# The first attention of a two-layer kernel rebuilt: weight look-up on TensorE, low parts of q and k made once and placed by DMA

## The reference, cut to what matters

```python
xt = jnp.transpose(x, (0, 2, 1))
q = xt @ Wq.T                                    # B, T=256, D=128; 8 heads of 16
qh = q.reshape(B, T, NH, dk).transpose(0, 2, 1, 3)
scores = scale * jnp.einsum('bhqd,bhkd->bhqk', qh, qh)
logits = (scores * cmask + (1.0 - cmask) * NEG) * rmask     # NEG = -1e30
attn = jax.nn.softmax(logits, axis=-1)
ctx = jnp.einsum('bhqk,bhkd->bhqd', attn, qh)
out = ctx.reshape(B, T, D) @ Wo.T                # transposed back, feeds the feed-forward
w = lut[idx]                                     # 16 entries; gate, up (688x256) and down (256x688)
h = silu(x @ w_gate.T) * (x @ w_up.T);  x = x + h @ w_down.T
```

## Time and profile before

| what | value |
|---|---|
| median of three runs | 783.47 us |
| profiled execution: time, span | 785.27 us, 783.5 us |
| PE, PEld busy | 628.1 us (80%), 364.8 us (47%) |
| DVE busy | 503.9 us (64%) |
| ACT, POOL busy | 373.6 us (48%), 214.3 us (27%) |
| mean granted clock of PE | 0.876 |

### The profile page before, as it was taken

The page is one execution under the profiler, slowest core; times in us unless marked ns, Lnnn a source line. Parts: engine busy times, 40 slices in busy tenths (PEclk is TensorE's granted clock), DMA queues, the critical chain, the costliest instruction groups (busy, mean ns, idle before and its releaser), DMA issues. The chain is left out here.

```text
span 783.5 us, 14597 instructions
## 1 busy us (share of the span) xinstructions
PE 628.1 (80%) x4411; PEld 364.8 (47%) x4443; DVE 503.9 (64%) x1050; ACT 373.6 (48%) x686; POOL 214.3 (27%) x243
## 2 busy tenths in 40 slices
PE   3588888787888879999956787788628999999993
PEld 1134444444444435555533454454414666666662
DVE  2589888999888875333336999999852333333331
ACT  1356766656766654243336777777502222222220
POOL 3444445665445532000000000000011233333221
PEclk9987666868676769999989999999858999999997
DMA  8200000000000000000036566655301111111110
GB/s 270 85 22 16 20 14 14 14 21 14 20 14 14 14 2 1 1 1 0 0 72 184 124 149 146 149 144 134 75 14 34 41 41 40 44 35 46 43 32 4
DMA packets 28252, 41.26 MB, mean 53 GB/s; under 512 B 6397, under 2 KB 17535, under 8 KB 28096
## 3 DMA queue, kind: packets, MB, share of 16 engines
q1 hardware_dynamic: 20752, 25.63, 11.0%
q0 software_dynamic: 5104, 13.39, 7.8%
q10 hardware_dynamic: 2368, 1.89, 0.8%
HBM read 40.88 MB, written 6.69 MB: 61 GB/s over the span
## 5 line engine op out<-in xcount | busy, mean ns | idle before, releaser
L524 ACT ACTIVATE probs<-PC 128x512 f32<-128x512 f32 x128 | 69.5, 598 | 63.7 <-PE PC L787 63.6
L1168 DVE TENSOR_REDUCE nmax<-PB 128x2 f32<-128x512 f32 x128 | 82.5, 666 | 24.9 <-PE PB L775 24.9
L1551 DVE TENSOR_TENSOR probs<-PC,probs 128x1024 bf16<-128x1024 f32 x19 | 23.3, 1225 | 81.0 <-ACT probs L721 81.0
L721 ACT CAST probs<-PC 128x1024 bf16<-128x1024 f32 x19 | 19.2, 1012 | 113.6 <-PE PC L1067 113.6
L439 POOL DMA_DIRECT2D arena<-in_w_all x16 | 8.5, 533 | 235.0 <-DVE arena L1405 137.9
L757 PE MATMUL PA<-small,wq 128*128 128x256 f32 x128 | 63.2, 588 | 11.2 <-DVE identb L1122 11.2
L384 POOL TENSOR_TENSOR small<-small,cst 128x512 bf16<-128x512 bf16 x32 | 39.6, 1237 | 117.6 <-PE PC L787 105.4
L537 ACT ACTIVATE arena<-arena,lutb,lutd 128x268 f32<-128x268 int32 x128 | 71.0, 610 | 0.0
L775 PE MATMUL PB<-small 64*128 64x256 bf16 x256 | 43.9, 336 | 23.7 <-DVE nmax L1168 20.4
L1059 PE MATMUL PA<-arena,probs 128*128 x227 | 53.5, 386 | 7.6 <-issue 3.5
L1078 PE MATMUL PD<-arena,probs 128*128 x456 | 54.6, 278 | 2.5 <-issue 2.5
(11 more groups left out here) (180 smaller groups left out, 1298.9 us busy)
## 6 DMA issues: line engine op xcount, KB each, us to landing
wst<-in_w_all SPq DMA_DIRECT2D x48, 256.0 KB, 2.8
arena<-in_w_all POOLq DMA_DIRECT2D x16, 384.0 KB, 6.0
arena<-in_idx_all SPq DMA_DIRECT2D x16, 134.0 KB, 2.2
small<-in_x SPq DMA_DIRECT2D x16, 128.0 KB, 2.1
tok_r<-rows SPq DMA_DIRECT2D x1, 2048.0 KB, 14.9
tok_x<-rows SPq DMA_DIRECT2D x16, 128.0 KB, 4.9
arena<-in_x SPq DMA_DIRECT2D x1, 1792.0 KB, 16.3
arena<-in_cond SPq DMA_DIRECT2D x1, 1792.0 KB, 19.9
```

The source lines that it names most:

```text
L524: nc.scalar.activation(probs[:, c, o], PC[:, o], ACT.Exp, scale=SCALE0).then_inc(S["ex"], 1)
L1168: v.tensor_reduce(nmax[:, c, s, :], PB[:, s * 512:(s + 1) * 512].rearrange("p (a k) -> p a k", k=T), AX.X, ALU.max, negate=True).then_inc( ...
```

## The change

Nothing is left out of the computation. Six things are done in another way:

1. **Stacks.** ACT copies PA straight into ks (with the constant column added) and into qs, both bf16 (`stacks`), behind all exponentials of the turn. DVE takes low = PA - qs once per half (`lows`). SP's DMAs then place every fourth row of low into qs (slot 2) and into ks (slot 1) and the mask row into ks (`patch`); rows are laid out in fours for it. `stack`, `keys` and the one-row matmul with its mask instruction on POOL go. PE's scores now wait for those DMAs (semaphores pt0, pt1).
2. **Look-up.** The indices are rounded to bf16 and written to memory once. For each piece of 256 columns (17 pieces, 17 x 256 = 4352) one DMA issued by ACT spreads them 16-fold over the partitions (`load_hot`, 1 MB in SBUF). One DVE instruction of 4096 columns turns them into ones and zeros (`one_hot`), 32 PE matmuls with 16 moving columns look up high and low part together (`look_up`), and one ACT copy stores both (`looked_up`). `bits`, `entries`, `select` and `table_parts` go.
3. **Masks** come row by row by DMA, two buffers, and no longer as one block.
4. **Order on PE.** The four projections of a turn stand in c = 2 and c = 3, the look-up behind c = 1, and the contexts are split in halves before and behind `max_rows`.
5. **Loads at the start.** Index and most of x on ACT's queue; the later layers' weights, which ACT issued at 1.4 to 10.5 us, are issued by POOL in its first turns.
6. **The feed-forward** waits for all 17 pieces, where it waited for the first 11 of 16.

The diff, cut to its core:

```diff
-            def keys(b, par, n):
-                nc.gpsimd.tensor_tensor(ks[:, par, o], A[:, o], cst[:, C_SK:C_SK + 1].broadcast_to([P, 512]), ALU.mult
-                                        ).then_inc(S["kh"], 1)
-                nc.gpsimd.tensor_tensor(ks[:, par, o], ks[:, par, o], q32[:, o], ALU.add).then_inc(S["kk"], 1)
...
+            def patch(b, par, h):                                  # SP
+                o = slice(h * 512, (h + 1) * 512)
+                sp.wait_ge(S["ka"], 2 * b + h + 1)
+                sp.dma_start(ks[ROW_ABSENT::64, par, o].rearrange("s (r t) -> s r t", t=T),
+                             absent_d[bass.ds(b, 1), :].unsqueeze(1).broadcast_to([2, 2, T])).then_inc(S[f"pt{h}"], 16)
+                sp.wait_ge(S["lo"], 2 * b + h + 1)
+                for t, slot in ((qs, 2), (ks, 1)):
+                    sp.dma_start(t[slot::4, par, o], low[slot::4, o]).then_inc(S[f"pt{h}"], 16)
...
+            pool.wait_ge(S["idx"], 16)
+            nc.gpsimd.tensor_copy(idxb, idx).then_inc(S["idxc"], 1)
+            pool.wait_ge(S["idxc"], 1)
+            pool.dma_start(idx_low.rearrange("g (v c) -> (g v) c", v=LUT), idxb).then_inc(S["idxs"], 16)
+            pool.wait_ge(S["idxs"], 16)
+            for c in range(2):
+                pool.dma_start(hot[:, c, :], hot_rows(c)).then_inc(S[f"hot_first{c}"], 16)
...
+            def stacks(b, par, h):                                 # ACT
+                nc.scalar.activation(ks[:, par, o], PA[:, o], ACT.Identity, bias=cst[:, C_EV:C_EV + 1]).then_inc(S["ka"], 1)
+                nc.scalar.copy(qs[:, par, o], PA[:, o]).then_inc(S["qa"], 1)
...
             def body(i, par, before=True, after=True):             # ACT
                 exps(i - 1, 0)
                 values(i - 1, 1 - par)
-                entries(i, par, 0)
                 exps(i - 1, 1)
-                entries(i, par, 1)
-                if after:
-                    round_q(i + 1, 0)
+                looked_up(i - 1)
+                load_hot(i + 1, 1 - par)
                 exps(i - 1, 2)
                 if before:
                     context_out(i - 2)
-                entries(i, par, 2)
                 exps(i - 1, 3)
                 if after:
-                    round_q(i + 1, 1)
-                entries(i, par, 3)
+                    stacks(i + 1, 1 - par, 0)
+                    stacks(i + 1, 1 - par, 1)
...
-                mm(PA[:, pr * T:(pr + 1) * T], wq3[:, pr].rearrange("p a b c -> p (a b c)"), xm[:, par, :], start=True, stop=False)
-                ins = mm(PA[:, pr * T:(pr + 1) * T], absent_row[:], absent[0:1, par, :], start=False, stop=True)
+                ins = mm(PA[:, pr * T:(pr + 1) * T], wq3[:, pr].rearrange("p a b c -> p (a b c)"), xm[:, par, :], start=True, stop=True)
...
             def scores(b, par, c, s):
-                pe.wait_ge(S["qk"], 2 * b + 1 + c // 2)
-                pe.wait_ge(S["kk"], 2 * b + 1 + c // 2)
+                pe.wait_ge(S[f"pt{c // 2}"], 48 * b + 48)
...
+            def look_up(c, par):
+                pe.wait_ge(S["onehot"], c + 1)
+                pe.wait_ge(S["q2"], min(c + 1, B) if isinstance(c, int) else c + 1)
+                bank = PD[:, 512:1024].rearrange("p (h c) -> p h c", h=2)
+                for j in range(LPC):
+                    ins = mm(bank[:, :, j * LG:(j + 1) * LG], hot[:, par, j * P:(j + 1) * P],
+                             lutw[:].rearrange("p h g -> p (h g)"), start=True, stop=True)
+                ins.then_inc(S["lmm"], 1)
...
-            def body(i, par, before=True, after=True):             # DVE
-                maxima(i, i - 1, 1 - par, before)
+                maxima(i, before)
                 if after:
-                    bits(i + 1, 1 - par)
-                    stack(i + 1, 1 - par)
+                    lows(i + 1, 1 - par, 0)
+                one_hot(i, par, half)
                 add_max(i, par)
+                if after:
+                    lows(i + 1, 1 - par, 1)
...
+                v.tensor_scalar(hot[:, par, :], hot[:, par, :], cst[:, C_V:C_V + 1], None, ALU.is_equal).then_inc(S["onehot"], 1)
+                v.tensor_tensor(low[:, o], PA[:, o], qs[:, par, o], ALU.subtract).then_inc(S["lo"], 1)
```

More of the change, by code:

```diff
@@ L48 @@
 NEWTON = 3
-C_R = C_ROWS + SLOTS
+C_V = C_ROWS + SLOTS
+C_G = C_V + 1
+C_R = C_G + LG
 C_T = C_R + P
@@ L529, in context_out, with looked_up, load_hot @@
                 nc.scalar.copy(c_out, PD[:, 512:512 + T]).then_inc(S["c"], 1)
-            def entries(c, par, part):
-                act.wait_ge(S["bit"], 4 * c + 4)
-                if not (isinstance(c, int) and c < 2):
-                    act.wait_ge(S["w0l"], c - 1)
-                for j in range(2 * part, 2 * part + 2):
-                    nc.scalar.activation(pick[:, par, j, :], bit[:, par, 0, :], ACT.Identity, scale=lutd[:, j:j + 1],
-                                         bias=lutb[:, 2 * j:2 * j + 1]).then_inc(S["entry"], 1)
-            act.wait_ge(S["ones"], 4)
-            for b in range(2):
-                for n in range(2):
-                    round_q(b, n)
-            act.wait_ge(S["lutd"], 1)
-            act.wait_ge(S["lut"], 16)
-            for part_ in range(4):
-                entries(0, 0, part_)
+            def looked_up(c):
+                act.wait_ge(S["lmm"], c + 1)
+                nc.scalar.copy(w0t[:, :, bass.ds(c * LCOLS, LCOLS)], PD[:, 512:1024].rearrange("p (h c) -> p h c", h=2)
+                               ).then_inc(S["w0"], 1)
+            def load_hot(c, par):
+                act.dma_start(hot[:, par, :], hot_rows(c)).then_inc(S[f"hot{par}"], 16)
+            for b in range(2):
+                for h in range(2):
+                    stacks(b, b, h)
+            act.wait_ge(S["ones"], 4)
             def body(i, par, before=True, after=True):
@@ L574, in _ @@
             exps(LAST, 1)
+            looked_up(LAST)
+            exps(LAST, 2)
             context_out(LAST - 1)
-            exps(LAST, 2)
             exps(LAST, 3)
+            for c in range(B, LCH):
+                looked_up(c)
             context_out(LAST)
@@ L856, in _ @@
                 if c == 1:
+                    look_up(LAST, 1)
                     outputs0(LAST - 1)
-            contexts(LAST, 1)
+            for c in range(B, LCH):
+                look_up(c, c % 2)
+            contexts(LAST, 1, 0)
+            contexts(LAST, 1, 1)
             def norm_and_router():
@@ L1157, in maxima, with table @@
-            def maxima(b, piece=None, par=0, before=False):
+            dve.wait_ge(S["cond"], 16)
+            v.tensor_scalar(absent, present, -1.0, 1.0, ALU.mult, ALU.add).then_inc(S["absent"], 1)
+            def table():
+                dve.wait_ge(S["lut"], 16)
+                v.tensor_copy(lutw[:, 0, 0:1], lutc[:, 0:1]).then_inc(S["lutl"], 1)
+                dve.wait_ge(S["lutl"], 1)
+                v.tensor_tensor(lutc[:, 1:2], lutc[:, 0:1], lutw[:, 0, 0:1], ALU.subtract).then_inc(S["lutl"], 1)
+                dve.wait_ge(S["lutl"], 2)
+                for h in range(2):
+                    v.tensor_scalar(lutw[:, h, :], cst[:, C_G:C_G + LG], lutc[:, h:h + 1], None, ALU.mult
+                                    ).then_inc(S["lutw"], 1)
@@ new lines, in one_hot, with lows @@
+            def one_hot(c, par, half):
+                if isinstance(c, int) and c < 2:
+                    dve.wait_ge(S[f"hot_first{c}"], 16)
+                else:
+                    dve.wait_ge(S[f"hot{par}"], 16 * half)
+                v.tensor_scalar(hot[:, par, :], hot[:, par, :], cst[:, C_V:C_V + 1], None, ALU.is_equal).then_inc(S["onehot"], 1)
+            def lows(b, par, h):
+                dve.wait_ge(S["qa"], 2 * b + h + 1)
+                unless_first(dve, S[f"pt{h}"], 48 * b)
+                o = slice(h * 512, (h + 1) * 512)
+                v.tensor_tensor(low[:, o], PA[:, o], qs[:, par, o], ALU.subtract).then_inc(S["lo"], 1)
@@ L1158, in maxima @@
+            def maxima(b, before=False):
                 for c in range(4):
                     for s in range(2):
-                        if piece is not None and s == 1:
-                            if c == 0:
-                                dve.wait_ge(S["entry"], 8 * piece + 8)
-                            elif c < 3:
-                                dve.wait_ge(S["pick"], 3 * piece + c)
                         dve.wait_ge(S["sa"], 8 * b + 2 * c + s + 1)
@@ L1171, in maxima @@
                             normalise(b - 2, 2 * c + s + 1)
-                    if piece is not None and c < 3:
-                        select(par, c + 1)
                 dve.wait_ge(S["max"], 8 * b + 8)
```

327 lines of the change are left out of this document (152 added, 175 removed), and 2 rows, old and new, of the table S.

## The result

The changed kernel takes 786.07 us in the median of 18 runs (782.84 to 790.72), the kernel before on the same chip 782.51 us (779.73 to 785.97): ratio 1.0051, 95% interval 1.0035 to 1.0067. It is slower by 0.5%; forecast were 771.5 us. The profiled execution, with a span of 781.2 us and 782.84 us in all, is the fastest of the 18, and that of before, at 785.27 us, was 2.8 us above the median of its 18, so the two traces by themselves differ by -2.3 us. They show where the gain stayed away, not the last half per cent.

The account below looks back on a forecast made before the run. PE bounds the loop at slow clock, DVE at fast. Periods of 16.1 us against 16.85 give -10 us over 13, first turns -2, tail 0: 785.3 becomes 773.3, less 1.8 is 771.5 us; range 747 to 797.

Parts of the forecast that it names:

- one load of 1 MB a period ... hidden unless it nears a period: Look-up load, issued a whole turn ahead: lands in some 6 to 13 us and costs the period nothing.
- 2.4 (bounds 2.0 and 4.0): Microseconds for the patch DMAs to land beside the 1 MB load, after 0.45 us for the first issue.
- rival D: Transfers bind: patches land after 4 us or more, or the comparison takes 4.3; 17.6 us a period, 793 us; chance 0.09.
- the new wait: PE waits for the patches before a turn's first scores: 2 us at 2.4 GHz, none at 1.2 GHz.
- My formula: Loop period from fast and slow periods weighted by clock share: 1/(0.46/13.5 + 0.54/19.3) = 16.1 us against 16.85.
- my slow period of 19.3: Loop period at 1.2 GHz, set by PE's work alone: 19.3 us, against 18.0 before.
- B: Rival: the clock holds; at 80% fast a period is 14.35 us, 749 us in all; chance 0.20.
- C: Rival: slow look-up and gap keep PE at 1.2 GHz; at 20% fast 17.7 us a period, 792 us; chance 0.18.
- E: Rival: at the start, hot rows come at 48 us instead of 38; 781 us; chance 0.08.
- DVE's work: DVE's busy time per loop period falls from 15.2 to 9.8 us, so DVE is no longer the bound.
- The first turns: Start of the kernel, with one_hot(0) at about 38 us (30 to 48): -2 us (-8 to +9).
- The look-up: 32 new PE matmuls a period, each loading 128 columns and moving 16: 2.2 us fast, 3.8 us slow.

Follow-up runs that it names:

- experiment 1: Changed kernel with the 1 MB look-up load's slowest dimension 16 instead of 8, so over 16 transfer engines: 732.37 us.
- Experiment 6: Changed kernel, load still on 8 engines, with nine unread f32 matmuls of 256 columns behind the contexts, where PE stands still: 780.52 us, ratio 0.9963.
- experiment 5: Kernel of experiment 1 with three f32 matmuls into an unread bank added behind the contexts: 716.16 us, ratio 0.9154.

## Why the prediction was wrong

**The step that failed** is "one load of 1 MB a period ... hidden unless it nears a period", and with it the landing of the patches at "2.4 (bounds 2.0 and 4.0)". With its 0.45 us for the first issue the forecast was 2.85 us from issue to scores, 4.45 at most. For patches that travel alone that was near (2.44 in experiment 1). Beside the load it is 5.1 us in the turn shown and 4.7 in the mean of the 13, and it is the load's end that sets it. I saw that the patches run beside the load and gave that 0.2 us (2.4 for the 2.2 of a 134 KB load), and asked of the load only when its own reader needs it. It also had to be gone before the patches, which are issued 7.4 us after it. On eight engines it needs 10. Priced as rival D (793 us, chance 0.09), this is what happened: the new wait came in every turn, 3.8 us in the mean where I had 2 at full clock and none at 1.2 GHz, and a period is 16.9 us for D's 17.6.

The Trainium skill ("DMA: Bandwidth & Descriptors", section "Queues, rings and completion order") says that each transfer engine takes turns between the queues that have work for it, a packet of several descriptors at a time. I did not weigh it. The runs agree that a load on one queue (ACT's) holds up patches on another (SP's); they don't show the size of a packet. The rule that I did cite, on slow dimensions below 16, holds: DMA share 0.50 with eight rows, 1.06 with sixteen. The estimate of 4.5 us (and 2 of fixed cost) that I took from that page for eight engines does not: measured are 9, from 199.9 to 208.9 us, and 10.4 from the issue.

**The sum, with measured terms.** With the mean wait of 3.8 us in place of 1.6 a full-clock period is 11.95 + 2.2 = 14.15. The clock's share is (0.71 - 0.5)/0.5 = 42%, inside my 38 to 56%. My formula with it and my slow period of 19.3 gives 1/(0.42/14.15 + 0.58/19.3) = 16.7; measured are 16.92. That agreement is luck. The 19.3 holds a look-up of 3.8 us where 1.0 was measured; with 16.5 in its place the formula gives 15.4. It also holds no wait at 1.2 GHz; with 3.8 us of wait there too it gives 17.2. Experiment 6 is a second reason for caution: at full clock beside the narrow load a turn took 14.3 to 16.1 us, most of them near 15.8, and no turn of the changed kernel ran at 1.2 GHz throughout, so the slow term was never measured by itself.

**Readings that were wrong.** I had the cast L1181 end in the same 10 ns as POOL's L388; by the earlier trace rows L388 ends at 187.55 and the cast at 187.61. That it is held up while POOL works still fits: the same cast (now L1189) takes 0.28 us in the mean with `keys` gone. I had the clock down at the next matmuls behind the gap of 1.27 us; in the trace the clock is 1.00 until 131.5 us, 0.9 us behind the gap, and 0.50 from there. And my count of the new wait lands at 13.3 us, while I wrote a period of 13.5.

**What held.** DVE's work: 10.5 us a period for 9.8. Comparison 1.28 for 1.3, a subtraction 0.69 for 0.66. L1189 is at 0.28 us in the mean, while L1187 is still held up (524 ns, at least 230), which is 0.3 of the difference. `one_hot(0)` at 39.3 us for 38, though it stands behind the first `add_max` (34.48 us) and not in front of it as I had counted. The first turns gave 2.8 us (54.45 for 57.28) for 2; the tail from the fifteenth `add_max` to the first matmul of the feed-forward is 24.16 us for 24.83, where I had no change.

**What was mis-sized without deciding.** The look-up: 0.9 us at full clock for 2.2, and 1.02 at clock 0.50 (at 197.24 us of the changed kernel) for 3.8. I had priced 16 moving columns by matmuls that move 128 and 256. The full-clock period without the meeting: 11.95 us for 13.5, with the wait at 1.6 for 2. The gain that I expected (12 us), and four times as much (732 us for 783), was there behind one transfer.

**Rivals.** B (clock holds) and C (clock stays low) did not come: 0.71 against 0.73. That a standstill takes the level down, the mechanism of C, is shown by the stretch of 206.83 to 211 us and by experiment 5. E did not come. I had called the chance of slower 0.29, too little of it on D.

**Left open.** Why the medians differ by +3.6 us while the profiled executions differ by -2.3: no trace of a median execution was compared. Why ten of 13 turns fall in experiment 1, and two when the load is left out, with similar waits. So how much of the 54 us is the shorter wait and how much the clock is not parted.

## What to carry to other kernels

Ask of a long transfer not only when its reader needs it but which short, urgent transfers it will meet, and let it end before them or start behind them. A slowest dimension of 16 instead of 8 halved it and took the median from 786 to 732 us. And a wait of PE at full clock can cost more than its length (turns of 13.5 to 16.0 us for 11.95 in experiment 1): where it can't be removed, try filling it, and look whether the clock or the transfer behind the wait is the limit (experiment 6).

## What was not expected of the hardware

- 1 MB in pieces of 8 KB took 9 us on eight transfer engines and 4.3 us on sixteen. 32 KB patches, 2.4 us from issue to use alone, took 5.1 us across the first in the turn shown and 4.8 across the second (over the loop 3.8 to 5.1, but for one turn of 7.0, and 4.7 to 5.4).
- Two patches are issued by SP in 1.12 us, 0.56 each, where I had 0.45 for the first.
- Matmuls with 16 moving columns, each with its own load of 128, follow one another in 28 ns (0.9 us / 32).
- Three unread f32 matmuls per turn, in a wait of 1.6 us, went with a clock of 0.99 in the profiled loop instead of 0.81 and with a median of 716 us instead of 732.
